# Expert tiles of 128 rows in a fused attention and mixture-of-experts kernel, with the first layer two tiles ahead

## The chip, the cores and the metric

The kernel runs on one core of a Trainium2 chip. The metric is the device time of one execution in microseconds (us), as the median of the runs shown. All data are fp32.

The core has five engines, each with its own instruction queue: TensorE (matmul, here PE, its weight loads PEld), VectorE (DVE), ScalarE (ACT), GpSimd (POOL) and SyncE (SP, which here issues transfers). They meet only through semaphores. Steps that a queue does itself (a wait, register arithmetic, a load of a register from memory) are listed in the trace under names such as DVEq.

## The reference, cut to what matters

The input x is (32, 256, 128). A linear-attention layer with a layer norm comes first, then a mixture of experts with a second layer norm:

```python
x = layernorm(x + attention(x, ...))
x_flat = x.reshape(8192, 128)
shared_out = relu(x_flat @ shared_w1 + b1) @ shared_w2 + b2        # 128 -> 512 -> 128
top_vals, top_idx = top_k(x_flat @ router_w + expert_bias, 2)
weights = softmax(top_vals)
comb = zeros((8192, 16)).at[rows, top_idx].add(weights)
for e in range(16):
    y_e = relu(x_flat @ w1[e] + b1[e]) @ w2[e] + b2[e]             # 128 -> 512 -> 128
    routed_out += comb[:, e:e+1] * y_e
x = layernorm(x + shared_out + routed_out)
```

## The kernel before, in words

**Three stages.** The first (0 to about 525 us) runs the attention, the router and the shared expert over 16 units of 512 tokens in a software pipeline whose order is written out by hand for each engine. GpSimd scatters each token's row twice, once for each chosen expert, into `dispatched_rows` in HBM, grouped by expert (L955). At its end VectorE's `make_table` turns the counts into a table of tiles: for each tile its expert (`tile_ei`) and its first row (`tile_ri`). The second, the **expert stage** (about 525 to 837 us), applies the experts tile by tile. The third (to the end) gathers the two results of each token, adds them and normalizes.

**A tile of the expert stage.** `ST` = 256 rows of one expert are a tile, in `SUB` = 2 halves of 128. Each expert's rows are rounded up to whole tiles, so there are always `ETILES` = 16384 / 256 + 16 = 80. For tile j:

- SyncE `load_rows` (L279 to L285) loads its rows into one of `RING` = 8 buffers: a `value_load` of the first row, then one DMA. It issues two tiles at a time once their earlier scatters are done.
- TensorE `e_turn` (L589) transposes it into PSUM; VectorE `e_xT` (L1269) copies that to SBUF.
- VectorE `e_w1` (L1273) reads the tile's expert number with a `value_load` (L1274) and copies that expert's first-layer weights and bias (128 x 516) into a ring of `W_RING` = 4, so that the matmuls and activations have fixed addresses.
- TensorE `e_up` (L595): 4 matmuls over 256 columns. ScalarE `e_hid` (L839): 4 activations, ReLU with bias, from PSUM to `hide`.
- TensorE `e_down` (L605): a `value_load` of the expert (L607), then 8 matmuls over 128 columns, 4 accumulated for each half.
- VectorE `e_y` (L1280): a `value_load` (L1281), a wait for `e_down` (L1282, L1283), then adds the bias b2. ScalarE `e_weigh` (L847) multiplies by the routing weight. GpSimd (L974 to L980) scatters the rows to `expert_results`, one indirect DMA for each half.

**The order.** Each engine's queue goes through its work in the order written. TensorE takes in step j: `e_turn`(j+2), `e_up`(j+1), `e_down`(j). ScalarE: `e_hid`(j+1), `e_weigh`(j). VectorE: `e_xT`(j+2), `e_w1`(j+3), `e_y`(j), in a loop of 4 steps; the last 4 tiles are written out after it. A `nop` with `nofuse` behind a wait keeps the wait a step of its own in the queue, which stops there; other waits ride on the instruction that follows.

Of the kernel before, what the change touches and what calls it, by code (L numbers as in the profile page):

```python
# [1411 lines left out]
```

## Time and profile before

| | us |
|---|---|
| median of 3 runs (range) | 891.84 (891.44 to 893.44) |
| the profiled execution, its own time | 892.41 |
| its span, first to last instruction | 890.3 |

The profile is of one execution. The span is a little shorter than the time. A row of the timeline gives the start, the time on the engine and, in brackets, how long the engine had been idle before it and what ended this. "issue" as the reason means that the engine waited for nothing that the profile shows. An fp32 matmul appears as two passes. Where a row carries a count, its time runs from the start of the first to the end of the last.

### The profile page before, as it was taken

To read this page: it belongs to the slowest core of one execution; us is meant where nothing else is said; L and a number is where in the kernel's file an instruction comes from. 1 tells how busy PE (TensorE), PEld (TensorE's weight loads), DVE (VectorE), ACT (ScalarE), POOL (GpSimd) and SP (SyncE) were. 2 spreads that over 40 slices of the span, in tenths; PEclk is the share of its full clock that TensorE was granted. 3 is DMA by queue.
4 is the path that set the end of the run, shared out by engine and by line. 5 is a ranking of instruction groups with operands and counts; after the bars stand their busy time and mean duration, and the time that the engine had idled before them with its cause. 6 is when DMAs were issued, how large, how long until landed. Compare 5 with 4: busy or idle time off the path is not lost. (4 is left out here: it accounts for less than half of the span.)

```text
span 890.3 us, 24269 instructions
## 1 busy us (share of the span) xinstructions
PE 785.1 (88%) x8068; PEld 568.6 (64%) x8069; DVE 494.6 (56%) x1496; ACT 489.7 (55%) x1153; POOL 556.4 (62%) x709
## 2 busy tenths in 40 slices
PE   4687999999999999999988769999999999999492
PEld 1243555555565556655555549999999999999340
DVE  2435777788787887788874423333333333333076
ACT  2343666556665567556663306666666666666247
POOL 5334687888878888788887534555555555555344
PEclk9966999999999999999998769999999999999796
DMA  4001012211122102221016221222222222221394
GB/s 164 24 2 43 19 47 65 68 53 31 54 69 64 53 26 62 68 62 56 26 39 204 87 69 41 73 71 67 72 69 65 65 66 63 67 67 40 114 316 138
DMA packets 70388, 63.44 MB, mean 71 GB/s; under 512 B 8066, under 2 KB 61704, under 8 KB 70176
## 3 DMA queue, kind: packets, MB, share of 16 engines
q1 hardware_dynamic: 60816, 44.99, 17.7%
q0 software_dynamic: 9216, 17.07, 5.8%
q8 instruction: 52, 0.85, 0.4%
q14 instruction: 32, 0.26, 0.1%
q10 hardware_dynamic: 272, 0.26, 0.1%
HBM read 38.75 MB, written 25.63 MB: 72 GB/s over the span
## 5 line engine op out<-in xcount | busy, mean ns | idle before, releaser
L979 POOL DMA_INDIRECT expert_results<-yw_all,rows x160 | 157.2, 983 | 155.2 <-ACT yw_all L851 130.5
L843 ACT ACTIVATE hide<-psB,w_ring 128x256 f32<-128x256 f32 x320 | 125.6, 475 | 65.1 <-PE psB L601 65.1
L612 PEld LDWEIGHTS psO<-w_sb,hide 128*128 128x128 f32 x1280 | 155.3, 192 | 4.6 <-issue 0.6
L612 PE MATMUL psO<-w_sb,hide 128*128 x1280 | 156.0, 275 | 0.1
L601 PE MATMUL psB<-x1T,w_ring 128*128 128x256 f32 x640 | 153.1, 382 | 0.2 <-DVE x1T L1271 0.2
L955 POOL DMA_INDIRECT dispatched_rows<-rows,slot x128 | 126.3, 986 | 38.8 <-issue 30.3
L1284 DVE TENSOR_TENSOR K<-psO,b_sb 128x256 f32<-128x256 f32 x80 | 34.0, 425 | 170.9 <-PE psO L612 170.9
L601 PEld LDWEIGHTS psB<-x1T,w_ring 128*128 128x128 f32 x640 | 116.4, 192 | 13.3 <-issue 0.6
L933 POOL TENSOR_TENSOR w_ring<-w_ring,tot 128x128 f32<-128x128 f32 (+2 forms) x160 | 116.8, 750 | 0.0
L851 ACT ACTIVATE yw_all<-K,rows 128x128 f32<-128x128 f32 x160 | 55.4, 393 | 67.5 <-DVE K L1284 67.5
L806 ACT ACTIVATE hide<-psO,cols 128x512 f32<-128x512 f32 x64 | 43.6, 682 | 75.6 <-PE psO L537 75.3
L537 PE MATMUL psO<-x1T,mats 128*128 128x512 f32 x128 | 73.2, 656 | 12.9 <-ACT hide L806 12.9
L1023 DVE SCALAR_TENSOR_TENSOR psP<-psP,cols,delta 128x512 f32<-128x512 f32 x80 | 60.3, 754 | 43.3 <-PE psP L328 43.3
L544 PEld LDWEIGHTS psO<-mats,hide 128*128 128x128 f32 x512 | 64.0, 204 | 20.5 <-issue 14.9
L544 PE MATMUL psO<-mats,hide 128*128 128x128 f32 x512 | 69.8, 294 | 2.2 <-ACT hide L806 2.2
L1034 DVE TENSOR_TENSOR mixed<-psP,hT 128x512 f32<-128x512 f32 x80 | 55.3, 692 | 15.0 <-PE psP L319 6.5
L940 POOL TENSOR_TENSOR o_rstd<-o_var,minus_half 128x16 f32<-128x16 f32 x16 | 46.9, 2931 | 26.8 <-DVE o_var L1077 26.8
L920 POOL TENSOR_TENSOR tot<-tot 128x128 f32<-128x128 f32 (+4 forms) x80 | 22.0, 275 | 62.5 <-ACT R_near L693 34.1
L439 PEld LDWEIGHTS psB<-w_ring,K 64*32 64x32 f32 x2048 | 20.5, 109 | 51.1 <-issue 49.5
L1278 DVE COPY w_ring<-w_sb 128x516 f32 x80 | 34.3, 429 | 29.8 <-issue 29.8
L439 PE MATMUL psB<-w_ring,K 64*32 64x64 f32 x2048 | 30.5, 229 | 20.2 <-POOL w_ring L933 20.0
L328 PE MATMUL psP<-adapt1a,mats 32*128 32x512 f32 x128 | 39.9, 700 | 6.6 <-issue 2.6
(173 smaller groups left out, 1314.9 us busy)
## 6 DMA issues: line engine op xcount, KB each, us to landing
rows<-dispatched_rows SPq DMA_DIRECT2D x80, 132.0 KB, 2.2
w_sb<-expert_results SPq DMA_DIRECT2D x8, 1024.0 KB, 11.9
h_res<-in_hidden SPq DMA_DIRECT2D x16, 256.0 KB, 3.4
out<-w_sb SPq DMA_DIRECT2D x16, 256.0 KB, 2.3
hT<-in_hidden_t SPq DMA_DIRECT2D x15, 256.0 KB, 3.9
w_sb<-in_w SPq DMA_DIRECT2D x14, 256.0 KB, 3.8
expert_results<-yw_all,rows POOLq DMA_INDIRECT x160, 2.3
dispatched_rows<-pad_rows SPq DMA_DIRECT2D x17, 132.0 KB, 3.7
```

The source lines that it names most:

```text
L439: last = mm(to, k, r, start=True, stop=True, tile_position=(64 * b, 32 * c4))
L537: mm(O1, mat("shared_w1")[:, c * 128:(c + 1) * 128], x1T[u % 2][:, :], start=True, stop=True).then_inc(sem(f"hid_ps{c}"))
L544: last = mm(O1[:, j * 128:(j + 1) * 128], hid[:, c, j * 128:(j + 1) * 128], mat("shared_w2")[:, c * 128:(c + 1) * 128], start=(c == 0), st ...
L601: last = mm(up_ps(p)[:, c // 2, (c % 2) * ST:(c % 2 + 1) * ST], w1b[i % W_RING][:, c * 128:(c + 1) * 128], xTe[p], start=True, stop=True)
L612: last = mm(psO[:, p, s * 128:(s + 1) * 128], hide[p][:, c, s * 128:(s + 1) * 128], w2_sb[:, bass.ds(e, 1), c, :].rearrange("p e c -> p (e ...
L843: last = A(hide[p][:, c, :], psB[:, 2 * p + c // 2, (c % 2) * ST:(c % 2 + 1) * ST], ACT.Relu, bias=w1b[i % W_RING][:, HIDDEN + c:HIDDEN + ...
L851: last = A(yw[i][:, s, :], ye[p][:, s, :], ACT.Copy, scale=row_in[i][:, s, AT_W:AT_W + 1])
L933: last = G.tensor_tensor(r, r, l, ALU.mult)
L955: G.indirect_dma_start(rows_dram[:, :], bass.IndirectOffsetOnAxis(slot[u % 2][:, j, k:k + 1], 0), rows[k][u % 2][:, j, :], None).then_inc( ...
L979: G.indirect_dma_start(back_dram[:, :], bass.IndirectOffsetOnAxis(row_in[i][:, s, AT_DEST:AT_DEST + 1].bitcast(u32), 0), yw[i][:, s, :], N ...
L1023: V.scalar_tensor_tensor(ps, ps, col(f"x_bias{n}"), delta[:, :, :], ALU.add, ALU.mult).then_inc(sem(f"mul{n}"))
L1034: V.tensor_tensor(mixed[MIX_BUF[n]][:, :, :], unflat(psP[MIX_BANK[n]]), hT[u % 2][:, :, 1:T + 1], ALU.add).then_inc(sem(f"mixed{n}"))
```

## The change

`ST` becomes 128, so a tile has one half, and there are 16384 / 128 + 16 = 144 tiles in place of 80. `RING` is 16, so the ring holds as many rows as before; rows are loaded, and their scatters counted, in groups of `GROUP` = 4 tiles. TensorE's order is now `e_turn`(j+3), `e_up`(j+2), `e_down`(j), ScalarE's `e_hid`(j+2), `e_weigh`(j); `hide`, `xTe` and `ye` have 4 buffers, and each tile's first layer has a PSUM bank of its own. ScalarE does three of the four chunks of the ReLU; the fourth is done by VectorE in a new `e_hid` behind ScalarE's three, with a semaphore of its own, `e_hid_v`, for which `e_down` and `e_w1` wait too. VectorE's order is `e_xT`(j+3), `e_w1`(j+4), `e_y`(j), `e_hid`(j+2). The table of tiles has two columns of 72 in place of one of 80, the padding rows written to HBM are 128 for each expert, and the load of b2 counts on the semaphore `late_weights`. The core of the diff (left out: shapes of the table's tiles and constants, the pads, that semaphore):

```diff
@@ -23,9 +23,9 @@
 NC = T // L
 HALVES = [2, 4, 8, 16]
 GROUPS = UB * NH // 2
-ST = 256
-SUB = ST // 128
-RING = 8
+ST = 128
+RING = 16
+GROUP = 4
 W_RING = 4
...
@@ -158,15 +158,15 @@
         slot_f = sb("slot_f", [128, TILES, TOPK])
         slot = two("slot", [128, TILES, TOPK], u32)
         dest = sb("dest", [128, TILES, TOPK])
-        hide_both = sb("hide", [128, 2, HC, ST])
-        hide = [hide_both[:, i, :, :] for i in range(2)]
-        hid = hide_both[:, :, :, :].rearrange("p i c t -> p (i c t)").rearrange("p (c t) -> p c t", t=UT)
+        hide_all = sb("hide", [128, 4, HC, ST])
+        hide = [hide_all[:, i, :, :] for i in range(4)]
...
-        tab = sb("tab", [128, 2])
-        yw_all = sb("yw_all", [128, RING, SUB, C])
+        past, past_row = sb("past", [128, 2, EXPERTS]), sb("past_row", [128, 2, EXPERTS])
+        tab = sb("tab", [128, 2, 2])
+        yw_all = sb("yw_all", [128, RING, C])
         tile_ei = sb("tile_ei", [1, ETILES], i32)
         tile_ri = sb("tile_ri", [1, ETILES], i32)
-        row_in = [r[:, i * SUB:(i + 1) * SUB, :] for r in (rows[0][0], rows[1][0], rows[1][1], rows[0][1]) for i in range(2)]
-        xTe = [x1T[0][:, i * ST:(i + 1) * ST] for i in range(2)]
-        ye = [K[i].rearrange("p (s c) -> p s c", c=C) for i in range(2)]
-        yw = [yw_all[:, i, :, :] for i in range(RING)]
+        row_in = [r[:, i, :] for r in (rows[0][0], rows[1][0], rows[1][1], rows[0][1]) for i in range(TILES)]
+        xTe = [x1T[0][:, i * ST:(i + 1) * ST] for i in range(4)]
+        ye = [K[i][:, j * C:(j + 1) * C] for i in range(2) for j in range(2)]
+        yw = [yw_all[:, i, :] for i in range(RING)]
 
...
@@ -278,22 +278,22 @@
 
             def load_rows(j, i):
                 if not (isinstance(j, int) and j < RING):
-                    sp.wait_ge(sem(f"e_back{i // 2}"), (j - i) * (2 * SUB * 16 // RING))
-                for t in range(2):
+                    sp.wait_ge(sem(f"e_back{i // GROUP}"), (j - i) * (GROUP * 16 // RING))
+                for t in range(GROUP):
                     sp.nop(nofuse=True)
                     r = sp.value_load(tile_ri[0:1, bass.ds(j + t, 1)], min_val=0, max_val=EXPERTS * CAP)
-                    sp.dma_start(row_in[i + t], rows_dram[bass.ds(r, ST), :].rearrange("(s p) c -> p s c", p=128)).then_inc(sem(f"e_rows_in{i // 2}"), 16)
+                    sp.dma_start(row_in[i + t], rows_dram[bass.ds(r, ST), :]).then_inc(sem(f"e_rows_in{i // GROUP}"), 16)
             done(sp, "base_out", UNITS - 2)
-            for j in range(0, RING, 2):
-                if j == RING - 2:
+            for j in range(0, RING, GROUP):
+                if j == RING - GROUP:
...
@@ -522,7 +522,8 @@
             def table_turn():
                 pe.wait_ge(sem("tab"), 1)
                 for i in range(2):
-                    last = nc.tensor.transpose(P0[0:1, i * 128:(i + 1) * 128], tab[:, i:i + 1], mat("ident"))
+                    for k in range(2):
+                        last = mm(P0[0:1, (2 * i + k) * (ETILES // 2):(2 * i + k + 1) * (ETILES // 2)], tab[:, i, k:k + 1], mat("ident")[:, 0:ETILES // 2], start=True, stop=True)
                 last.then_inc(sem("tab_ps"))
 
             def f_up(u, c):
...
@@ -584,48 +585,44 @@
             pe.wait_ge(sem("expert_weights"), (UNITS - 1) * 16)
             pe.wait_ge(sem("b2_ready"), 1)
             pe.wait_ge(sem("tile_table"), 1)
-            up_ps = lambda p: psB[:, 2 * p:2 * p + 2, :]
 
             def e_turn(j, i):
-                pe.wait_ge(sem(f"e_rows_in{i // 2}"), (j - i) * (32 // RING) + 32)
-                for s in range(SUB):
-                    last = nc.tensor.transpose(psP[i % 2][:, s * 128:(s + 1) * 128], row_in[i][:, s, 0:C], mat("ident"))
-                last.then_inc(sem("e_turn_ps"))
+                pe.wait_ge(sem(f"e_rows_in{i // GROUP}"), (j - i) * (GROUP * 16 // RING) + GROUP * 16)
+                nc.tensor.transpose(psP[i % 2][:, 0:ST], row_in[i][:, 0:C], mat("ident")).then_inc(sem("e_turn_ps"))
 
             def e_up(j, i):
-                p = i % 2
                 pe.wait_ge(sem("e_xT"), j + 1)
                 pe.wait_ge(sem("e_w1"), j + 1)
                 pe.nop(nofuse=True)
                 for c in range(HC):
-                    last = mm(up_ps(p)[:, c // 2, (c % 2) * ST:(c % 2 + 1) * ST], w1b[i % W_RING][:, c * 128:(c + 1) * 128], xTe[p],
-                              start=True, stop=True)
+                    last = mm(psB[:, i % 4, c * ST:(c + 1) * ST], w1b[i % W_RING][:, c * 128:(c + 1) * 128], xTe[i % 4], start=True, stop=True)
                 last.then_inc(sem("e_up_ps"))
 
             def e_down(j, i):
-                p = i % 2
                 e = pe.value_load(tile_ei[0:1, bass.ds(j, 1)], min_val=0, max_val=EXPERTS - 1)
                 pe.wait_ge(sem("e_hid"), j + 1)
-                pe.nop(nofuse=True)
-                for s in range(SUB):
-                    for c in range(HC):
-                        last = mm(psO[:, p, s * 128:(s + 1) * 128], hide[p][:, c, s * 128:(s + 1) * 128],
-                                  w2_sb[:, bass.ds(e, 1), c, :].rearrange("p e c -> p (e c)"), start=(c == 0), stop=(c == HC - 1))
+                pe.wait_ge(sem("e_hid_v"), j + 1)
+                pe.nop(nofuse=True)
+                for c in range(HC):
+                    last = mm(psO[:, i % 2, 0:C], hide[i % 4][:, c, :], w2_sb[:, bass.ds(e, 1), c, :].rearrange("p e c -> p (e c)"),
+                              start=(c == 0), stop=(c == HC - 1))
                 last.then_inc(sem("e_down_ps"))
 
             e_turn(0, 0)
             e_turn(1, 1)
             e_up(0, 0)
+            e_turn(2, 2)
+            e_up(1, 1)
             with pe.Fori(0, ETILES // RING - 1) as ring:
                 for i in range(RING):
-                    e_turn(pe.snap(ring * RING + (i + 2)), (i + 2) % RING)
-                    e_up(pe.snap(ring * RING + (i + 1)), (i + 1) % RING)
+                    e_turn(pe.snap(ring * RING + (i + 3)), (i + 3) % RING)
+                    e_up(pe.snap(ring * RING + (i + 2)), (i + 2) % RING)
                     e_down(pe.snap(ring * RING + i), i)
             for j in range(ETILES - RING, ETILES):
+                if j + 3 < ETILES:
+                    e_turn(j + 3, (j + 3) % RING)
...
@@ -837,28 +834,24 @@
 
 
             def e_hid(j, i):
-                p = i % 2
                 act.wait_ge(sem("e_up_ps"), j + 1)
-                for c in range(HC):
-                    last = A(hide[p][:, c, :], psB[:, 2 * p + c // 2, (c % 2) * ST:(c % 2 + 1) * ST], ACT.Relu,
-                             bias=w1b[i % W_RING][:, HIDDEN + c:HIDDEN + c + 1])
+                for c in range(HC - 1):
+                    last = A(hide[i % 4][:, c, :], psB[:, i % 4, c * ST:(c + 1) * ST], ACT.Relu, bias=w1b[i % W_RING][:, HIDDEN + c:HIDDEN + c + 1])
                 last.then_inc(sem("e_hid"))
 
             def e_weigh(j, i):
-                p = i % 2
                 act.wait_ge(sem("e_y"), j + 1)
-                for s in range(SUB):
-                    last = A(yw[i][:, s, :], ye[p][:, s, :], ACT.Copy, scale=row_in[i][:, s, AT_W:AT_W + 1])
-                last.then_inc(sem("e_yw"))
+                A(yw[i], ye[i % 4], ACT.Copy, scale=row_in[i][:, AT_W:AT_W + 1]).then_inc(sem("e_yw"))
 
             e_hid(0, 0)
+            e_hid(1, 1)
             with act.Fori(0, ETILES // RING - 1) as ring:
                 for i in range(RING):
-                    e_hid(act.snap(ring * RING + (i + 1)), (i + 1) % RING)
+                    e_hid(act.snap(ring * RING + (i + 2)), (i + 2) % RING)
...
@@ -975,9 +967,8 @@
                 for i in range(RING):
                     pool.wait_ge(sem("e_yw"), ring * RING + (i + 1))
                     pool.nop(nofuse=True)
-                    for s in range(SUB):
-                        G.indirect_dma_start(back_dram[:, :], bass.IndirectOffsetOnAxis(row_in[i][:, s, AT_DEST:AT_DEST + 1].bitcast(u32), 0),
-                                             yw[i][:, s, :], None, bounds_check=TRASH - 1, oob_is_err=False).then_inc(sem(f"e_back{i // 2}"), 16)
+                    G.indirect_dma_start(back_dram[:, :], bass.IndirectOffsetOnAxis(row_in[i][:, AT_DEST:AT_DEST + 1].bitcast(u32), 0),
+                                         yw[i], None, bounds_check=TRASH - 1, oob_is_err=False).then_inc(sem(f"e_back{i // GROUP}"), 16)
 
...
@@ -1266,42 +1259,49 @@
             dve.wait_ge(sem("b2_ready"), 1)
 
 
-            def e_xT(j, p):
+            def e_xT(j, i):
                 dve.wait_ge(sem("e_turn_ps"), j + 1)
-                V.tensor_copy(xTe[p], psP[p][:, 0:ST]).then_inc(sem("e_xT"))
+                V.tensor_copy(xTe[i % 4], psP[i % 2][:, 0:ST]).then_inc(sem("e_xT"))
 
             def e_w1(j, i):
                 e = dve.value_load(tile_ei[0:1, bass.ds(j, 1)], min_val=0, max_val=EXPERTS - 1)
                 if not (isinstance(j, int) and j < W_RING):
                     dve.wait_ge(sem("e_hid"), j + (1 - W_RING))
+                    dve.wait_ge(sem("e_hid_v"), j + (1 - W_RING))
                 dve.nop(nofuse=True)
                 V.tensor_copy(w1b[i % W_RING][:, :], w1_sb[:, bass.ds(e, 1), :].rearrange("p e n -> p (e n)")).then_inc(sem("e_w1"))
 
-            def e_y(j, p):
+            def e_hid(j, i):
+                dve.wait_ge(sem("e_hid"), j + 1)
+                c = HC - 1
+                V.tensor_scalar(hide[i % 4][:, c, :], psB[:, i % 4, c * ST:(c + 1) * ST], w1b[i % W_RING][:, HIDDEN + c:HIDDEN + c + 1], 0.0,
+                                ALU.add, ALU.max).then_inc(sem("e_hid_v"))
+
+            def e_y(j, i):
                 e = dve.value_load(tile_ei[0:1, bass.ds(j, 1)], min_val=0, max_val=EXPERTS - 1)
                 dve.wait_ge(sem("e_down_ps"), j + 1)
                 dve.nop(nofuse=True)
-                V.tensor_tensor(ye[p], psO[:, p, 0:ST].rearrange("p (s c) -> p s c", c=C),
-                                b2_sb[:, bass.ds(e, 1), :].broadcast_to([128, SUB, C]), ALU.add).then_inc(sem("e_y"))
+                V.tensor_tensor(ye[i % 4], psO[:, i % 2, 0:C], b2_sb[:, bass.ds(e, 1), :].rearrange("p e c -> p (e c)"), ALU.add).then_inc(sem("e_y"))
 
             dve.wait_ge(sem("w1_in"), 4 * 16)
-            for j in range(3):
+            for j in range(W_RING):
                 e_w1(j, j)
-                if j < 2:
+                if j < 3:
                     e_xT(j, j)
+            e_hid(0, 0)
+            e_hid(1, 1)
             with dve.Fori(0, ETILES // W_RING - 1) as quad:
                 for i in range(W_RING):
-                    dve.wait_ge(sem("e_up_ps"), quad * W_RING + (i + 1))
-                    e_xT(dve.snap(quad * W_RING + (i + 2)), i % 2)
-                    e_w1(dve.snap(quad * W_RING + (i + 3)), (i + 3) % W_RING)
-                    e_y(dve.snap(quad * W_RING + i), i % 2)
+                    e_xT(dve.snap(quad * W_RING + (i + 3)), i + 3)
+                    e_w1(dve.snap(quad * W_RING + (i + 4)), i)
+                    e_y(dve.snap(quad * W_RING + i), i)
+                    e_hid(dve.snap(quad * W_RING + (i + 2)), i + 2)
             for j in range(ETILES - W_RING, ETILES):
+                if j + 3 < ETILES:
+                    e_xT(j + 3, j + 3)
+                e_y(j, j)
                 if j + 2 < ETILES:
-                    dve.wait_ge(sem("e_up_ps"), j + 1)
-                    e_xT(j + 2, j % 2)
-                if j + 3 < ETILES:
-                    e_w1(j + 3, (j + 3) % W_RING)
-                e_y(j, j % 2)
+                    e_hid(j + 2, j + 2)
 
 
             def f_add(u):
```

## Rows read from the trace of the kernel before

**Rows 1.** The page's first part: busy time, share of the span, instructions.
```profile
PE 785.1 (88%) x8068; PEld 568.6 (64%) x8069; DVE 494.6 (56%) x1496; ACT 489.7 (55%) x1153; POOL 556.4 (62%) x709
```

**Rows 2.** Stages: stretch, us, busy PE, PEld, DVE, ACT, POOL, clock, DMA, GB/s.
```profile
0.00:400.00 400.00, 348.24 (x4717) 204.61 (x4718) 288.27 (x805) 224.05 (x488) 286.87 (x402) 0.96 0.18 54
...
480.00:500.00 20.00, 15.17 (x104) 9.15 (x94) 10.86 (x50) 6.08 (x12) 10.36 (x10) 0.65 0.56 185
...
600.00:700.00 100.00, 100.00 (x698) 94.45 (x698) 32.21 (x80) 60.68 (x162) 52.81 (x54) 1.00 0.24 68
```

**Rows 3.** Groups, 520 to 820 us: count, busy us, mean ns, idle before and releaser.
```profile
L979 POOL DMA_INDIRECT expert_results<-yw_all,rows x151 | 148.4, 983 | 149.2 <-ACT yw_all L851 126.3 <-issue 22.8
...
L843 ACT ACTIVATE hide<-psB,w_ring 128x256 f32<-128x256 f32 x309 | 121.4, 475 | 64.0 <-PE psB L601 64.0
...
L1278 DVE COPY w_ring<-w_sb 128x516 f32 x80 | 34.3, 429 | 29.8 <-issue 29.8
...
L1284 DVE TENSOR_TENSOR K<-psO,b_sb 128x256 f32<-128x256 f32 x76 | 32.3, 425 | 160.9 <-PE psO L612 160.9
```

**Rows 4.** The timeline, TensorE, one tile: start us, us, instruction.
```profile
642.22 0.38 PE L592 MATMUL psP<-mats,rows 128*128 128x128 f32 x2
642.44 1.89 PE L601 MATMUL psB<-x1T,w_ring 128*128 128x256 f32 x8
644.17 1.95 PE L612 MATMUL psO<-w_sb,hide 128*128 x16
645.95 0.38 PE L592 MATMUL psP<-mats,rows 128*128 128x128 f32 x2
```

**Rows 5.** The timeline, VectorE, one turn of its loop.
```profile
601.53 0.42 DVE L1284 TENSOR_TENSOR K<-psO,b_sb 128x256 f32<-128x256 f32 x1 [2.08 <-PE psO L612]
...
602.57 0.43 DVE L1278 COPY w_ring<-w_sb 128x516 f32 x1 [0.28 <-issue]
...
609.00 0.42 DVE L1284 TENSOR_TENSOR K<-psO,b_sb 128x256 f32<-128x256 f32 x1 [2.28 <-PE psO L612]
...
610.47 0.43 DVE L1278 COPY w_ring<-w_sb 128x516 f32 x1 [0.47 <-issue]
612.73 0.42 DVE L1284 TENSOR_TENSOR K<-psO,b_sb 128x256 f32<-128x256 f32 x1 [1.83 <-PE psO L612]
...
613.95 0.43 DVE L1278 COPY w_ring<-w_sb 128x516 f32 x1 [0.47 <-issue]
```

**Rows 6.** VectorE's queue by line, 601.3 to 604 us: ns min/median/max, first and last start.
```profile
L1274 DVEq TENSOR_LOAD <-tile_ei x1: 310/310/310, 601.8 to 601.8; - x1
L1274 DVEq FUSED_REGOPS  x2: 53/122/190, 601.7 to 602.1; - x2
L1281 DVEq TENSOR_LOAD <-tile_ei x1: 302/302/302, 602.7 to 602.7; - x1
L1281 DVEq SEQ_ASSERT  x1: 23/23/23, 603.2 to 603.2; - x1
L1283 DVEq EVENT_SEMAPHORE  x1: 21/21/21, 601.4 to 601.4; - x1
```

**Rows 7.** The timeline at the expert stage's start and end.
```profile
529.17 1.09 PE L592 MATMUL psP<-mats,rows 128*128 128x128 f32 x4 [4.43 <-DMA rows<-dispatched_rows]
...
538.10 0.42 DVE L1284 TENSOR_TENSOR K<-psO,b_sb 128x256 f32<-128x256 f32 x1 [2.50 <-PE psO L612]
...
831.06 0.42 DVE L1284 TENSOR_TENSOR K<-psO,b_sb 128x256 f32<-128x256 f32 x1 [1.69 <-PE psO L612]
...
834.78 0.98 POOL L979 DMA_INDIRECT expert_results<-yw_all,rows  x1 [0.31 <-issue]
836.96 15.57 SPq L300 DMA_DIRECT2D w_sb<-expert_results  x7
```

**Rows 8.** SyncE's row loads by line, 525 to 535 us.
```profile
L285 SPq DMA_DIRECT2D rows<-dispatched_rows x8: 377/378/388, 525.7 to 533.8; - x8
```

**Rows 9.** The chain that ended last: the routing stage's last scatter.
```profile
522.37 2.28 DMA dispatched_rows<-rows,slot
```

More of the change, by code:

```diff
@@ L39 @@
 MIX_BUF = {n: i % 2 for i, n in enumerate(MIX_ORDER)}
-COLS = (["x_mu", "router_b", "xl_b2a", "xl_b2b"] + [f"x_bias{n}" for n in range(NMIX)] + ["w_b", "bonus", "gn_w", "gn_b", "tile_no", "tile_row", "head0", "head1", "head2", "head3"]
+COLS = (["x_mu", "router_b", "xl_b2a", "xl_b2b"] + [f"x_bias{n}" for n in range(NMIX)] + ["w_b", "bonus", "gn_w", "gn_b", "tile_no0", "tile_no1", "tile_row0", "tile_row1", "head0", "head1", "head2", "head3"]
         + [f"shared_b1_{c}" for c in range(HC)])
@@ L246, in _ @@
             load_h(1)
-            sp.dma_start(b2_sb[:, :, :], b2_dram).then_inc(sem("b2_in"), 16)
+            sp.dma_start(b2_sb[:, :, :], b2_dram).then_inc(sem("late_weights"), 16)
             sp.wait_ge(sem("pad_rows"), 1)
             def write_pad(e):
-                sp.dma_start(rows_dram[e * CAP:e * CAP + ST, :].rearrange("(s p) c -> p s c", p=128), pad_rows[:, :, :]).then_inc(sem("padded"), 16)
+                sp.dma_start(rows_dram[e * CAP:e * CAP + ST, :], pad_rows[:, :]).then_inc(sem("padded"), 16)
             write_pad(EXPERTS)
@@ L291, in _ @@
             with sp.Fori(0, ETILES // RING - 1) as ring:
-                for i in range(0, RING, 2):
+                for i in range(0, RING, GROUP):
                     load_rows(sp.snap(ring * RING + (i + RING)), i)
-            for q in range(RING // 2):
-                sp.wait_ge(sem(f"e_back{q}"), ETILES // RING * 2 * SUB * 16)
+            for q in range(RING // GROUP):
+                sp.wait_ge(sem(f"e_back{q}"), ETILES // RING * GROUP * 16)
             for q in range(UNITS // 2):
@@ L894, in _ @@
                     G.memset(rows[k][p][:, :, :], 0.0)
-            G.memset(pad_rows[:, :, :], 0.0)
+            G.memset(pad_rows[:, :], 0.0)
             G.memset(v_flat[0], 0.0)
@@ L1184, in make_table @@
                 link(V.tensor_tensor_scan(tiles_to[:, :], ones_row[:, :], tiles_f[:, :], 0.0, ALU.mult, ALU.add))
-                V.tensor_scalar(past[:, :], tiles_to[:, :], col("tile_no"), None, ALU.is_le)
+                for k in range(2):
+                    V.tensor_scalar(past[:, k, :], tiles_to[:, :], col(f"tile_no{k}"), None, ALU.is_le)
                 link(V.tensor_tensor(first_row[:, 0:EXPERTS], counts[:, :], mat("region"), ALU.add))
@@ L1188, in make_table @@
                 link(V.tensor_tensor(row_step[:, :], first_row[:, 1:EXPERTS + 1], first_row[:, 0:EXPERTS], ALU.subtract))
[L1189 to L1194 removed]
+                link(V.tensor_tensor(past_row[:, :, :], past[:, :, :], row_step[:, :].unsqueeze(1).broadcast_to([128, 2, EXPERTS]), ALU.mult))
+                V.tensor_reduce(tab[:, 0, :], past[:, :, :], AX.X, ALU.add)
+                link(V.tensor_reduce(tab[:, 1, :], past_row[:, :, :], AX.X, ALU.add))
+                V.scalar_tensor_tensor(tab[:, 1, 0:1], tab[:, 1, 0:1], col("tile_row0"), first_row[:, 0:1], ALU.add, ALU.add)
+                link(V.scalar_tensor_tensor(tab[:, 1, 1:2], tab[:, 1, 1:2], col("tile_row1"), first_row[:, 0:1], ALU.add, ALU.add))
+                V.tensor_scalar(tab[:, 0, :], tab[:, 0, :], float(EXPERTS - 1), None, ALU.min)
+                V.tensor_scalar(tab[:, 1, :], tab[:, 1, :], float(EXPERTS * CAP), None, ALU.min).then_inc(sem("tab"))
                 dve.wait_ge(sem("tab_ps"), 1)
                 V.tensor_copy(tile_ei[:, :], P0[0:1, 0:ETILES])
[L1197 removed]
+                V.tensor_copy(tile_ri[:, :], P0[0:1, ETILES:2 * ETILES]).then_inc(sem("tile_table"))
             def c_slots(u):
@@ L1384, in pack @@
     putc("gn_b", g("gn_bias"))
-    putc("tile_no", p.astype(np.float32))
-    putc("tile_row", p.astype(np.float32) * ST)
+    for k in range(2):
+        putc(f"tile_no{k}", (p + k * (ETILES // 2)).astype(np.float32))
+        putc(f"tile_row{k}", (p + k * (ETILES // 2)).astype(np.float32) * ST)
     for n in range(NH):
```

26 lines of the change are left out of this document (8 added, 18 removed).

## Prediction

> **What bounds the kernel now.** I read the page's busy table first: TensorE is busy 785 us of 890, VectorE 495 [rows 1]. A whole-span share says little here, so next comes the table by stage. In the expert stage, 600 to 700 us, TensorE is busy 100.00 of 100 us at granted clock 1.00 and VectorE only 32.21 us [rows 2]. The groups of that stage say who waits: VectorE's L1284 waited 160.9 us for TensorE, ScalarE's L843 64.0 us, and GpSimd's scatter L979 126.3 us for ScalarE [rows 3]. TensorE alone sets the pace. Its timeline shows the pace: from one L592 to the next, 642.22 to 645.95, is 3.73 us for a tile of 256 rows [rows 4]. The first `e_y` starts at 538.10 and the 80th at 831.06, so 79 steps take 292.96 us [rows 7], 3.71 each.
>
> **TensorE's share of the change.** One step splits in rows 4 into 0.22 us for two transposes, 1.73 for the 8 passes of `e_up` over 256 columns (an fp32 matmul is two passes), and 1.78 for the 16 passes of `e_down` over 128 columns: 0.111 us for a pass over 128. The new tile of 128 rows has 1 + 8 + 8 = 17 such passes, 17 x 0.111 = 1.89 us. 144 x 1.89 = 272 us stands against 80 x 3.73 = 298 us: fewer padded rows, 26 us less. If TensorE stayed the bound, that would be the gain. But the tile period falls by half, so I ask what each other engine does once for a tile, whatever its size.
>
> **VectorE's queue, the term that decides.** VectorE's busy time for a new tile is small: 0.43 for the copy of `w1`, and below the 256-column 0.42 each for `e_xT`, `e_y` and the new ReLU, under 1.7 us together [rows 3, 5]. The idle time ahead of L1278 is marked "issue", 29.8 us in 80 [rows 3]: nobody was waited for; the queue itself was busy. I therefore laid out what the queue does for a tile. Clearing the wait of L1283 comes at 601.4, the addition starts at 601.53: 0.16 us with the register step between them (an estimate within the tenths of the rows) [rows 5, 6]. From there to the start of the `w1` copy one step of a loop turn takes 1.04 us, the next as much (not shown), then come 1.47 and 1.22 [rows 5], mean 1.19. They hold the issue of `e_xT` and one `value_load` with its register work: L1274 begins at 601.7, of it 310 ns for the load and 190 ns for the register work behind it [rows 6]. The 1.47 is the step with the loop's branch. From the copy's start (602.57) the second `value_load`, L1281, follows at once and ends with the assertion at 603.2 plus 23 ns [rows 5, 6]; with the gap to the next instruction that is 0.72 us. Sum: 0.16 + 1.19 + 0.72 = 2.07 us that the queue is at work for each tile, none of it dependent on the number of rows. Today it hides in the 3.73 us step, and the queue then stands still 2 us until the next `e_down` is done (idle 1.83 to 2.28 before L1284) [rows 5].
>
> In the changed kernel all of it stays: both `value_load`s, the waits, the loop turn every 4 tiles. Added is the ReLU of the fourth chunk with a wait on a computed count. No row shows that instruction. The nearest is the issue of `e_xT`, an instruction with such a wait: between the addition's start at 601.53 and L1274's first step at 601.7 [rows 5, 6]. That bounds it by 0.10 and 0.20; I take 0.11, since the computed count and the issue are all it adds. From below: zero, if it disappeared in a gap. The wait on `e_up_ps` goes and the second wait of `e_w1` comes, which I put at nothing together (at most one more wait of 21 ns plus its gap, as L1283 in rows 6). So 2.18 us a tile, from 2.07 to 2.40. This is above TensorE's 1.89, so **VectorE's queue becomes the bound** and TensorE waits about 0.3 us in each tile.
>
> Does the order of the work let it run at 2.18? Copying xT(j+2) opens VectorE's step j-1. `e_up` (j+2) can begin about 0.5 us after it, `e_up` and `e_down` take 1.8, so `e_down`(j) is done some 2.5 us after the start of that step; VectorE asks for it in step j, at 2.18 + 0.1 + 0.9 + 0.7 = 3.9. ScalarE has in between one `e_weigh` and three activations, none above the 0.48 of L843's over 256 columns [rows 3], so below 1.9 us in all. So no wait of VectorE's queue comes late, and two tiles of lead are what makes that so. Behind the new ReLU's wait for ScalarE the next `e_xT` is queued, and by this count ScalarE is done a good microsecond before.
>
> **The rest has cover.** GpSimd now scatters once a tile instead of twice: 983 ns plus 0.30 of issue [rows 3, 7] is 1.29, under 2.18. SyncE loads each tile with one DMA; eight take 525.7 to 533.8, 1.16 us each [rows 8], under 2.18; should GpSimd or SyncE be late, each would still have 0.9 us of slack a tile. The rows are refilled in groups of 4 out of 16, which leaves SyncE about 9 tiles between a group's last scatter and its need. The table of tiles has three more small VectorE operations and two more matmuls; SyncE waits for the last scatter of the routing stage (522.37 to 524.65) [rows 9] anyway, so I put them at 0 and at 0.5 us if that cover were gone. Pads of half the size, and the load of `b2` now awaited ahead of the first `c_attn`, are at 0: those ends lie in the first stage, which TensorE fills 87% [rows 2], with tens of microseconds between load and need.
>
> **Ends of the stage.** Start: the first transpose now waits for 4 loads, not 2: 2 x 1.16 = +2.3 us [rows 8]. From first transpose (529.17) to first `e_y` (538.10) are 8.93 us [rows 7]; the new fill has four `w1` copies and three xT ahead of the ReLU, which at 0.75 a pair, half-clock `e_up`s of 1.8 and one queue turn give about 8.0: -0.9. End: from the last `e_y` to the landed last scatter are 831.06 to 836.96, 5.90 us, since GpSimd still owes three scatters [rows 7]. Then, one weighing (0.4, within L843's 0.48), one scatter's delay and its 2.2 us to landing, with 0.4 of backlog: about 4.3, -1.6. Net of the ends: -0.2.
>
> **Sum.** The last four tiles have no `w1` copy and take about 5.0 us together, the 139 before them 139 x 2.18 = 303.0: 308.0 against 292.96, +15.0. With the ends +14.8. The profiled execution took 892.41 us (span 890.3 and 2.1 around it), so 907.2; it stands 0.57 above the median of the runs shown, so I forecast **906.6 us**, 1.6% slower.
>
> **A rule against the row.** L1274's load of a register from SBUF takes 310 ns here and L1281's 302 [rows 6]. The Trainium skill, page "DMA: Bandwidth & Descriptors", section "Latency and other measured facts", gives `tensor_load` a floor of about 600 ns. By that figure, an estimate from the page, the two loads of a tile would add another 0.6 us. The trace disagrees with the page in all steps of the steady stage.
>
> **Rivals.** (A) TensorE stays the bound: the queue work overlaps more than I think, or is issued ahead, and a tile takes 1.89. Then 139 x 1.89 + 4.9 = 267.6, -25.4, with the ends 866. For it speaks that VectorE is busy only a third of the stage; against it that the queue's steps in rows 5 and 6 are strictly one after the other. It decides when the queue's work falls below 1.89. Chance 0.12; another 0.04 lies between 1.89 and 2.06, where the time is still below today's. (B) Slower for more queue work: the ReLU costs 0.20, and the two waits and longer loops add 0.1 more, 2.40 a tile: 139 x 2.40 + 5 = 338.6, 937. It speaks for it that one step in four already takes 0.2 more for no visible reason (613.95 - 612.73 against 1.04) [rows 5]. Chance 0.08. (C) The clock: TensorE's gaps bring it to the low level. Between 480 and 500 it was busy 76% and had a mean clock of 0.65; between 0 and 400 it was busy 87%, as it would be now (1.89 of 2.18), at 0.96 [rows 2]. At 0.96 its step is 1.97, still under 2.18. At the low level it is 3.8; a tenth of the tiles there cost 14 x 1.6 = 22 us more, 929. Chance 0.05. (D) By a mechanism of this kernel, the loads of registers slow down when VectorE works without pause: taking instead of 0.31 us the 0.6 us, 2.78 a tile, gives 139 x 2.78 + 5 = 391, some 990 us. Rows 6 show no sign of it, though VectorE was busy during both loads. This is where the page named above would put it. Chance 0.01.
>
> **How the numbers follow.** Today's time is met at (292.96 + 0.2 - 5) / 139 = 2.07 us a tile. My forecast's own case, 2.07 to 2.36, holds 0.67: 891 to 932. What I call no change (0.2%, about what a measurement of this kernel can tell) is 2.06 to 2.085 and holds 0.03 of all. Faster: A and the stretch under 2.06, 0.16. Slower: 0.81. The range for 8 in 10 takes in a little of the stretch below, and C and the lower part of B above: 890 to 933.
>
> **What would show it.** Right: in the stage VectorE's groups have idle time by "issue", and L1284's successor waits little for TensorE; TensorE is busy near 87% with gaps ahead of the first layer that end on VectorE's xT; the tile period is 2.1 to 2.3 us, with every fourth longer. Wrong: TensorE busy 100% at 1.89 (A); a queue period over 2.4 (B); granted clock under 0.95 (C); register loads far from 305 ns (D); or ScalarE's activations named as what ends the idle time, which would mean that my count of slack in the order of the work is false.

## The result, and the profile after

| | before | after |
|---|---|---|
| median, us (runs) | 891.92 (4) | 906.62 (4), 906.04 to 908.62 |
| ratio, 95% interval | | 1.0166, 1.0145 to 1.0186 |
| profiled execution: time, span | 892.41, 890.3 | 906.18, 904.3 |
| expert stage, first to last `e_y` | 292.96 for 80 tiles | 309.25 for 144 tiles |

The changed kernel is slower by 14.7 us. 906.6 was forecast, in a range of 890 to 933.

I read the stage first, as in [rows 2]. The first line is of the kernel after (stretch, us, busy PE, PEld, DVE, ACT, POOL, clock, DMA, GB/s):

```profile
600.00:700.00 100.00, 97.21 (x776) 90.50 (x775) 54.81 (x184) 53.69 (x184) 45.64 (x46) 1.00 0.21 59
```

By this line alone one would still name TensorE. The groups of the same stretch, VectorE, say otherwise (in [rows 3] L1284 waited for TensorE):

```profile
L1272 DVE COPY w_ring<-w_sb 128x516 f32 x46 | 20.2, 440 | 22.4 <-issue 14.5 <-ACT hide L839 7.9
L1277 DVE TENSOR_SCALAR hide<-psB,w_ring 128x128 f32<-128x128 f32 x46 | 15.7, 342 | 0.0
L1284 DVE TENSOR_TENSOR K<-psO,b_sb 128x128 f32<-128x128 f32 x46 | 13.4, 292 | 22.8 <-issue 22.8
L1264 DVE COPY x1T<-psP 128x128 f32<-128x128 f32 x46 | 13.0, 282 | 0.0
```

All idle time ahead of `e_y` (L1284) is now "issue": it waits neither for TensorE nor for anyone, and the queue comes to it late. VectorE's data path is busy 55% of the time, but its queue sets the pace. Its timeline, a turn of its loop, where [rows 5] showed the one before:

```profile
651.95 0.29 DVE L1284 TENSOR_TENSOR K<-psO,b_sb 128x128 f32<-128x128 f32 x1 [0.57 <-issue]
652.16 0.34 DVE L1277 TENSOR_SCALAR hide<-psB,w_ring 128x128 f32<-128x128 f32 x1
652.42 0.28 DVE L1264 COPY x1T<-psP 128x128 f32<-128x128 f32 x1
653.26 0.43 DVE L1272 COPY w_ring<-w_sb 128x516 f32 x1 [0.56 <-issue]
654.17 0.29 DVE L1284 TENSOR_TENSOR K<-psO,b_sb 128x128 f32<-128x128 f32 x1 [0.48 <-issue]
...
656.15 0.29 DVE L1284 TENSOR_TENSOR K<-psO,b_sb 128x128 f32<-128x128 f32 x1 [0.47 <-issue]
...
658.12 0.29 DVE L1284 TENSOR_TENSOR K<-psO,b_sb 128x128 f32<-128x128 f32 x1 [0.47 <-issue]
...
659.65 0.48 DVE L1272 COPY w_ring<-w_sb 128x516 f32 x1 [0.72 <-ACT hide L839]
660.68 0.29 DVE L1284 TENSOR_TENSOR K<-psO,b_sb 128x128 f32<-128x128 f32 x1 [0.56 <-issue]
```

From one `e_y` to the next are 2.22, 1.98, 1.97 and 2.56 us, mean 2.18. The long one holds the loop's branch. Between the rows the queue is at work: in all 118 tiles of 560 to 820 us the step that clears the wait for TensorE (L1283) starts 48 to 50 ns behind the step before it, where in the kernel before it starts 1.40 to 1.95 us behind. The queue's own lines for 600 to 700 us (ns min/median/max) have about the same durations as [rows 6]:

```profile
L1267 DVEq TENSOR_LOAD <-tile_ei x46: 300/309/402, 599.8 to 698.2; - x46
L1281 DVEq FUSED_REGOPS  x92: 53/122/190, 600.8 to 699.4; - x92
L1281 DVEq TENSOR_LOAD <-tile_ei x46: 298/302/315, 600.9 to 699.1; - x46
L1281 DVEq SEQ_ASSERT  x46: 23/23/23, 601.5 to 699.7; - x46
```

The page's chain that ended last has moved there too:

```profile
PE 37%; issue 15%; DVEq 14%; POOL 13%; DVE 13%; ACT 5%; DMA 2%; SPq 0%; POOLq 0%; ACTq 0%
DVEq L1281 8%; PE psO L545 6%; POOL w_ring L925 6%; PE psP L328 5%; PE psB L439 4%; DVEq L1267 3%; POOL dispatched_rows L947 3%; ACT hide L839 3%; PE psB L481 3%; DVE hide L1277 3%; PE psP L319 3%; DVE K L1284 2%; POOL K L914 2%; PE psP L343 2%; PE psB L459 2%
```

A load of one register (L1281) is the costliest line of the chain, at 8% of the span.

**Why TensorE looks 97% busy.** Its timeline in the kernel after:

```profile
652.30 0.27 PE L591 MATMUL psP<-mats,rows 128*128 128x128 f32 x1
652.84 1.13 PE L598 MATMUL psB<-x1T,w_ring 128*128 128x128 f32 x8 [0.28 <-DVE x1T L1264]
653.82 1.15 PE L607 MATMUL psO<-w_sb,hide 128*128 x8
654.81 0.27 PE L591 MATMUL psP<-mats,rows 128*128 128x128 f32 x1
```

The transpose starts at 652.30 and the first layer at 652.84, 0.54 later, where passes in a row follow at 0.11. The array started nothing for 0.43 us beyond one pass, but of the 0.54 the rows count 0.27 as the transpose, whose end is modelled, and only the rest as idle. The rows that tell are the distances from start to start. The wait ends on VectorE's copy of xT, as forecast.

The ends of the stage, after (for [rows 7]):

```profile
530.12 0.66 PE L591 MATMUL psP<-mats,rows 128*128 128x128 f32 x2 [7.18 <-DMA rows<-dispatched_rows]
...
538.33 0.29 DVE L1284 TENSOR_TENSOR K<-psO,b_sb 128x128 f32<-128x128 f32 x1 [0.85 <-issue]
...
847.59 0.29 DVE L1284 TENSOR_TENSOR K<-psO,b_sb 128x128 f32<-128x128 f32 x1 [0.99 <-PE psO L607]
...
849.13 0.98 POOL L970 DMA_INDIRECT expert_results<-yw_all,rows  x1 [0.30 <-issue]
...
851.33 2.87 SPq L300 DMA_DIRECT2D w_sb<-expert_results  x3
```

### The profile page after: what moved, and what is told of

It reads as the page before. It is cut to its first block, busy times and chain, and to the rows that moved or that the text cites. A ratio compares the mean times of both kernels' runs of the same rounds, so it can differ in the third digit from the quotient of the medians.

```text
span 904.3 us, 27677 instructions
## 1 busy us (share of the span) xinstructions
PE 787.7 (87%) x8442; PEld 570.5 (63%) x8443; DVE 571.0 (63%) x1834; ACT 477.4 (53%) x1249; POOL 542.8 (60%) x693
## 4 chain that ended last, share of the span: by engine, by line
PE 37%; issue 15%; DVEq 14%; POOL 13%; DVE 13%; ACT 5%; DMA 2%; SPq 0%; POOLq 0%; ACTq 0%
DVEq L1281 8%; PE psO L545 6%; POOL w_ring L925 6%; PE psP L328 5%; PE psB L439 4%; DVEq L1267 3%; POOL dispatched_rows L947 3%; ACT hide L839 3%; PE psB L481 3%; DVE hide L1277 3%; PE psP L319 3%; DVE K L1284 2%; POOL K L914 2%; PE psP L343 2%; PE psB L459 2%
## 5 line engine op out<-in xcount | busy, mean ns | idle before, releaser
L970 POOL DMA_INDIRECT expert_results<-yw_all,rows x144 | 143.7, 998 | 184.1 <-ACT yw_all L844 174.0
L598 PE MATMUL psB<-x1T,w_ring 128*128 128x128 f32 x1152 | 160.2, 283 | 8.8 <-DVE x1T L1264 8.1
L607 PE MATMUL psO<-w_sb,hide 128*128 x1152 | 164.4, 286 | 0.4 <-ACT hide L839 0.2
L598 PEld LDWEIGHTS psB<-x1T,w_ring 128*128 128x128 f32 x1152 | 141.2, 193 | 23.8 <-issue 22.3
L607 PEld LDWEIGHTS psO<-w_sb,hide 128*128 128x128 f32 x1152 | 139.5, 191 | 5.8 <-issue 1.2
L844 ACT ACTIVATE yw_all<-K,rows 128x128 f32<-128x128 f32 x144 | 57.9, 402 | 144.8 <-DVE K L1284 144.8
L839 ACT ACTIVATE hide<-psB,w_ring 128x128 f32<-128x128 f32 x432 | 124.5, 357 | 16.9 <-PE psB L598 16.7
L1272 DVE COPY w_ring<-w_sb 128x516 f32 x144 | 63.3, 440 | 69.5 <-issue 44.2
L1284 DVE TENSOR_TENSOR K<-psO,b_sb 128x128 f32<-128x128 f32 x144 | 42.0, 292 | 73.4 <-issue 70.0
L1277 DVE TENSOR_SCALAR hide<-psB,w_ring 128x128 f32<-128x128 f32 x144 | 49.2, 342 | 1.1 <-ACT hide L839 1.0
```

The source lines that it names most:

```text
L598: last = mm(psB[:, i % 4, c * ST:(c + 1) * ST], w1b[i % W_RING][:, c * 128:(c + 1) * 128], xTe[i % 4], start=True, stop=True)
L607: last = mm(psO[:, i % 2, 0:C], hide[i % 4][:, c, :], w2_sb[:, bass.ds(e, 1), c, :].rearrange("p e c -> p (e c)"), start=(c == 0), stop=(c ...
L839: last = A(hide[i % 4][:, c, :], psB[:, i % 4, c * ST:(c + 1) * ST], ACT.Relu, bias=w1b[i % W_RING][:, HIDDEN + c:HIDDEN + c + 1])
L970: G.indirect_dma_start(back_dram[:, :], bass.IndirectOffsetOnAxis(row_in[i][:, AT_DEST:AT_DEST + 1].bitcast(u32), 0), yw[i], None, bounds_ ...
L1272: V.tensor_copy(w1b[i % W_RING][:, :], w1_sb[:, bass.ds(e, 1), :].rearrange("p e n -> p (e n)")).then_inc(sem("e_w1"))
L1277: V.tensor_scalar(hide[i % 4][:, c, :], psB[:, i % 4, c * ST:(c + 1) * ST], w1b[i % W_RING][:, HIDDEN + c:HIDDEN + c + 1], 0.0, ALU.add, A ...
```

## The experiments

The theory: VectorE's queue, at 2.18 us a tile whatever a tile holds, sets the pace. Rivals: TensorE, whose busy share is 97%; ScalarE's chain, which the trace names as one releaser; VectorE's data path or the wait of its new ReLU. The table collects what the traces of all kernels show. The column "a tile" is the mean distance of two `e_y` in the steady part. `e_turn`, `e_up` and `e_down` of a tile are 17 passes of TensorE at 0.11 us, 1.89 us if nothing holds them up.

| kernel | us (runs) | a tile, us | first to last `e_y` |
|---|---|---|---|
| before | 891.92 (4) | 3.73 | 292.96 |
| after | 906.6 (4) | 2.18 | 309.25 |
| held | 865.61 (4) | 1.90 | 268.82 |
| no_load_y | 863.37 (1) | 1.90 | 268.67 |
| relu_act | 892.82 (10) | 2.09 | 296.48 |
| short_down | 906.24 (1) | 2.18 | 308.14 |
| extra_load | 997.00 (1) | 2.82 | 397.95 |
| before_extra_load | 891.73 (10) | 3.73 | 292.97 |
| held_relu_act | 865.27 (4) | 1.90 | 269.05 |
| one_ahead | 868.27 (4) | 1.90 | 271.82 |
| held_short_down | 823.76 (1) | 1.62 | 228.72 |
| before_short_down | 810.84 (1) | 2.72 | 212.38 |

**held: one of the two loads goes.** The expert's number is the same in `e_w1`(j) and `e_y`(j), four steps apart, and the loop has four steps, so a register can carry it.

```diff
+            held = [dve.alloc_register(f"held{i}") for i in range(W_RING)]
...
             def e_y(j, i):
-                e = dve.value_load(tile_ei[0:1, bass.ds(j, 1)], min_val=0, max_val=EXPERTS - 1)
+                e = dve.snap(held[i % W_RING], min_val=0, max_val=EXPERTS - 1)
...
-                e_w1(j, j)
+                dve.reg_mov(held[j], e_w1(j, j))
...
-                    e_w1(dve.snap(quad * W_RING + (i + 4)), i)
+                    e = e_w1(dve.snap(quad * W_RING + (i + 4)), i)
                     e_y(dve.snap(quad * W_RING + i), i)
+                    dve.reg_mov(held[i], e)
```

> The changed kernel, but the expert number that the copy of w1 reads for tile j+4 is kept in one of four registers, and the addition of b2 takes it from there four steps later in place of a load of its own. Queue theory (VectorE's queue sets 2.19 us a tile): a load and its register work, 0.63 to 0.73 us, go, two register moves of about 0.1 together come, so the queue needs 1.6; TensorE's 17 passes of 1.89 us then bound. 139 x (2.19 - 1.89) = 42 us less: 865, from 863 to 872. Rival, VectorE's data path or the wait of its new ReLU for ScalarE is what holds it: no change, 905 to 908. Rival, TensorE is the bound already (its busy share in the stage is 97%): at most 3% of 309 us, 897 or more.

Measured: 865.61 us (863.33 to 866.43), ratio to before 0.9696 (0.9672 to 0.9720). It falls by 41.0 us from the changed kernel, where 42 was worked out. The trace shows TensorE at work without a gap, 1.89 us from transpose to transpose, and now `e_y` waiting for it (the stretch's line, TensorE's timeline, then VectorE's):

```profile
600.00:700.00 100.00, 100.00 (x900) 100.00 (x899) 62.08 (x211) 67.50 (x212) 51.74 (x54) 1.00 0.24 67
```
```profile
652.38 0.27 PE L591 MATMUL psP<-mats,rows 128*128 128x128 f32 x1
652.49 1.06 PE L598 MATMUL psB<-x1T,w_ring 128*128 128x128 f32 x8
653.38 1.06 PE L607 MATMUL psO<-w_sb,hide 128*128 x8
654.27 0.27 PE L591 MATMUL psP<-mats,rows 128*128 128x128 f32 x1
```
```profile
654.64 0.29 DVE L1287 TENSOR_TENSOR K<-psO,b_sb 128x128 f32<-128x128 f32 x1 [0.32 <-PE psO L607]
```

Nothing is left out of this kernel, and it is faster than both given ones, by 26 us and by 41. The edit takes no work from VectorE's data path, from ScalarE, GpSimd or SyncE, and leaves the new ReLU with its wait for ScalarE as it was. So neither the data path nor that wait held the changed kernel at 2.18.

**no_load_y: the same load left out, without the register moves.**

```diff
             def e_y(j, i):
-                e = dve.value_load(tile_ei[0:1, bass.ds(j, 1)], min_val=0, max_val=EXPERTS - 1)
...
-                V.tensor_tensor(ye[i % 4], psO[:, i % 2, 0:C], b2_sb[:, bass.ds(e, 1), :].rearrange("p e c -> p (e c)"), ALU.add).then_inc(sem("e_y"))
+                V.tensor_tensor(ye[i % 4], psO[:, i % 2, 0:C], b2_sb[:, 0, :], ALU.add).then_inc(sem("e_y"))
```

> The changed kernel where the addition of b2 uses expert 0's row for every tile, so that VectorE reads no expert number for it (left out: the bias of the right expert). Queue theory: 1.45 us a tile in the queue, TensorE's 1.89 bounds: 865, from 863 to 870, and as fast as the variant that keeps the number in a register. Rivals as there: no change for VectorE's data path or ScalarE, 897 or more for TensorE.

Measured: 863.37 us in one run; its stage is as long as held's (268.67 against 268.82). With the load gone TensorE bounds both, and the register moves are hidden.

**relu_act: the quarter of the ReLU back on ScalarE.**

```diff
-                for c in range(HC - 1):
+                for c in range(HC):
                     last = A(hide[i % 4][:, c, :], ...)
...
                 pe.wait_ge(sem("e_hid"), j + 1)
-                pe.wait_ge(sem("e_hid_v"), j + 1)
+                if isinstance(j, int) and j + 2 >= ETILES:
+                    pe.wait_ge(sem("e_y"), j - 1)
...
-                    dve.wait_ge(sem("e_hid_v"), j + (1 - W_RING))
...
-                    e_hid(dve.snap(quad * W_RING + (i + 2)), i + 2)
```

The added wait for `e_y` is in the last two tiles alone.

> The changed kernel with the fourth chunk of the ReLU back on ScalarE; VectorE has no ReLU and no wait on it. Queue theory: the issue of the ReLU, its computed count and the second semaphore of the w1 copy go, 0.07 to 0.12 us a tile, 139 times: 890 to 897. ScalarE then works 4 x 0.27 + 0.4 = 1.5 us a tile, still under 2.07. Rival, ScalarE's chain (activations, then weighing) sets the pace: 0.27 us longer a tile, 940. Rival, TensorE: no change, 906.

Measured: 892.82 us, ratio to before 1.0006 (0.9994 to 1.0019): 13.8 us less than the changed kernel, 0.10 us for each of 144 tiles (0.09 by the distances of `e_y`). Moving work from ScalarE to VectorE, with the semaphore that it needs, is what the changed kernel pays these 14 us for. ScalarE with 69% of its time busy sets no pace. The stage's line and VectorE's groups:

```profile
600.00:700.00 100.00, 99.77 (x813) 94.68 (x812) 44.99 (x144) 68.55 (x239) 49.57 (x48) 1.00 0.21 62
```
```profile
L1272 DVE COPY w_ring<-w_sb 128x516 f32 x48 | 20.6, 430 | 28.8 <-issue 28.8
L1284 DVE TENSOR_TENSOR K<-psO,b_sb 128x128 f32<-128x128 f32 x48 | 14.0, 292 | 24.2 <-issue 24.2
```

Here the line has TensorE busy 99.77% and its weight loads 94.68%, yet a tile takes 2.09 us, where 1.89 is what TensorE needs, as held shows. The counts in the same line say it: 813 passes in 100 us here, 900 in held. And the releaser "ACT hide L839" ahead of the copy is gone, with the step that it stood in, the one with the branch, shorter by 0.07 (2.49 against 2.57, medians), though ScalarE now has more to do. In the changed kernel, too, the queue's step that clears the copy's waits (L1271) always starts 46 to 50 ns behind the step before it. ScalarE had been named as the last of several semaphores and did not hold the copy up.

**short_down: TensorE's work cut by a third.**

```diff
-                for c in range(HC):
+                for c in range(HC - 1, HC):
                     last = mm(psO[:, i % 2, 0:C], hide[i % 4][:, c, :], w2_sb[:, bass.ds(e, 1), c, :].rearrange("p e c -> p (e c)"),
-                              start=(c == 0), stop=(c == HC - 1))
+                              start=True, stop=True)
```

> The changed kernel where the second layer multiplies one of its four chunks alone (left out: three quarters of the second layer's products), so TensorE has 11 passes a tile, 1.22 us, in place of 17, 1.89. Queue theory: no change, 904 to 908, since TensorE waits for VectorE. Rival, TensorE (97% busy in the stage) sets the pace: 0.67 us less a tile, 139 times, 813.

Measured: 906.24 us. Six of 17 passes of each tile are left out and the time stays; TensorE's gaps grow instead:

```profile
600.00:700.00 100.00, 74.08 (x505) 61.21 (x506) 54.86 (x183) 53.58 (x184) 45.84 (x46) 1.00 0.20 59
```

The rival that TensorE sets the pace falls.

**extra_load and before_extra_load: the dose the other way.** The same line added to both kernels.

```diff
                 e = dve.value_load(tile_ei[0:1, bass.ds(j, 1)], min_val=0, max_val=EXPERTS - 1)
+                dve.value_load(tile_ei[0:1, bass.ds(j, 1)], min_val=0, max_val=EXPERTS - 1)
```

> The changed kernel with one more load of the expert's number, unused, on VectorE ahead of the addition of b2 in each tile. Queue theory: its full 0.6 to 0.7 us come on top of each tile's 2.18: 144 x 0.65 = 94 us more, 995 to 1005. Rivals (data path, ScalarE, TensorE): hidden, 906.

> The kernel before with the same additional unused load on VectorE ahead of the addition of b2. There the queue stands still 1.8 us a tile, so all theories that name VectorE's queue as covered in the kernel before expect no change: 891 to 893. If the loads disturbed TensorE or the engine's data in another way, each of 80 tiles would show it: up to 80 x 0.65 = 52 us more.

Measured: 997.00 us for the changed kernel, 90.4 more, 0.63 us a tile; 891.73 for the kernel before, ratio 0.9993 (0.9973 to 1.0014), no change. The queue's lines of the added load in extra_load:

```profile
L1282 DVEq TENSOR_LOAD <-tile_ei x35: 297/304/305, 601.7 to 697.9; - x35
L1282 DVEq FUSED_REGOPS  x35: 190/190/190, 602.0 to 698.2; - x35
L1282 DVEq SEQ_ASSERT  x35: 23/23/23, 602.3 to 698.5; - x35
```

304 + 190 + 23 ns and the gaps between make up the 0.63. In the kernel before the queue stands still 1.84 us a tile (median), and with the added load 1.21: the same steps fill part of a wait. This cover for the queue's work is there in the kernel before, and it is what small tiles take away.

**held_relu_act and one_ahead: what the other two parts of the change are worth.** held_relu_act is held with relu_act's edit. one_ahead goes back in addition to one tile of lead on TensorE, ScalarE and VectorE:

```diff
-                    e_turn(pe.snap(ring * RING + (i + 3)), (i + 3) % RING)
-                    e_up(pe.snap(ring * RING + (i + 2)), (i + 2) % RING)
+                    e_turn(pe.snap(ring * RING + (i + 2)), (i + 2) % RING)
+                    e_up(pe.snap(ring * RING + (i + 1)), (i + 1) % RING)
...
-                    e_hid(act.snap(ring * RING + (i + 2)), (i + 2) % RING)
+                    e_hid(act.snap(ring * RING + (i + 1)), (i + 1) % RING)
...
-                    e_xT(dve.snap(quad * W_RING + (i + 3)), i + 3)
+                    e_xT(dve.snap(quad * W_RING + (i + 2)), i + 2)
```

> The variant that keeps the expert number in a register, with the fourth chunk of the ReLU back on ScalarE. There TensorE's 1.89 us a tile is the bound. Queue theory: VectorE's queue falls from about 1.65 to 1.55 us a tile, which is hidden: 865.6 as before, 863 to 868. Rival, ScalarE needs the relief: it then has 4 x 0.27 + 0.4 = 1.5 us of work a tile and waits on two engines in turn; if that chain is longer than 1.89, 2.1 us a tile, 894.

> The same (number kept in a register, ReLU on ScalarE), with the first layer one tile ahead as in the kernel before, in place of two. Between the end of e_up(j) and the start of e_down(j) TensorE still has e_down(j-1), a transpose and e_up(j+1), 1.89 us; ScalarE needs 0.15 + 1.2 for the activations in between. If that holds the second tile of lead is worth nothing: 865, 863 to 868. Rival, with small tiles one tile of lead is too short, since ScalarE gets to the activations late, behind its weighing: TensorE would stand still 0.3 us or more a tile, 907 or more.

Measured: 865.27 us (ratio 0.9693, 0.9669 to 0.9717) and 868.27 us (0.9721, 0.9688 to 0.9753). With TensorE as the bound the ReLU's place is of no account: ScalarE did not need the relief. One tile of lead holds 1.90 us a tile in the steady part. Its stage is 2.8 us longer, of which 1.7 fall on the last four tiles (7.26 against 5.53); the medians' intervals overlap. So two tiles of lead are worth about 3 us by the medians, which these runs can't tell from nothing, and the rival's 40 are excluded.

**before_short_down and held_short_down: the same cut where TensorE is the bound.** The edit is short_down's, in the kernel before on both halves.

> The kernel before where the second layer multiplies one of its four chunks alone (left out: three quarters of the second layer's products): TensorE has 16 - 12 = 4 passes of e_down a tile, 1.34 us less of 3.73. There TensorE is the bound, so the time must fall, until GpSimd's two scatters of 1.29 us a tile bound at 2.6: 79 x (3.73 - 2.6) = 89 us less, 803; down to 787 if GpSimd kept up. The same cut left the changed kernel where it was (906.24). Rival, VectorE's queue or ScalarE already set the pace in the kernel before: no change, 892.

> The variant that keeps the expert number in a register, with the same cut of the second layer (left out: three quarters of its products): TensorE 11 passes, 1.22 us a tile. There the bound is TensorE's 1.89, and beneath it lies VectorE's queue at about 1.55 to 1.7. So a fall to the queue's own time: 139 x (1.894 - 1.62) = 38 us less, 828, from 817 to 838. If nothing but TensorE bounded it, 139 x 0.67 = 93 us less, 772. If the queue still bound it at 1.89, no change, 865.

Measured: 810.84 and 823.76 us, each in one run. The kernel before falls by 81 us, so TensorE did set its pace; I had put the new bound at 2.6 us a tile and it was 2.72. The trace shows the scatters back to back on GpSimd for long stretches, with TensorE waiting for rows at times (us in total, times, longest, 560 to 720 us). That GpSimd is the bound here is read from these rows; no run tests it:

```profile
641.61 0.98 POOL L979 DMA_INDIRECT expert_results<-yw_all,rows  x1 [0.30 <-issue]
642.89 0.98 POOL L979 DMA_INDIRECT expert_results<-yw_all,rows  x1 [0.30 <-issue]
644.18 0.99 POOL L979 DMA_INDIRECT expert_results<-yw_all,rows  x1 [0.30 <-issue]
```
```profile
PEld psP L592 <- DMA rows<-dispatched_rows: 16.9, 26, 2.3
PE psP L592 <- DMA rows<-dispatched_rows: 11.6, 20, 2.1
```

held falls from 1.90 to 1.62 us a tile and no further: that is the time of its queue with one load (2.18 less 0.63, with the moves), where 1.62 was put on record. The 1.22 that TensorE and its 11 passes would have allowed is not reached. The queue again waits for nobody: the steps that clear its waits (L1273, L1286) start 46 to 51 ns behind the ones before them.

## Why the prediction was right

| term | forecast | measured |
|---|---|---|
| a tile | 2.18 | 2.18 |
| first to last `e_y` | +15.0 | +16.3 |
| first load to first transpose | +2.3 | +1.9 |
| first transpose to first `e_y` | -0.9 | -0.7 |
| last `e_y` to the gather | -1.6 | -2.2 |
| before the first load | 0 | -0.9 |
| after the gather | 0 | -0.4 |
| span | +14.8 | +14.0 |

**The queue's work for a tile** was summed from the steps of its own rows: 2.07, and 0.11 for the new ReLU. It is 2.18. The parts of the 0.11 were not quite those that I named. The ReLU with all that hangs on it costs 0.09 to 0.10 (relu_act). Without it the sum from [rows 5, 6] is 2.07, and 2.09 is measured, so the two terms miss by 0.02 each way and cancel. Rival D is excluded: a load takes 298 to 315 ns at L1281 in a queue that never rests. The load with all its register work took 0.63 us in extra_load. The floor of about 600 ns that the Trainium skill gives for `tensor_load` (page "DMA: Bandwidth & Descriptors", section "Latency and other measured facts") doesn't agree with these rows as the time of the load itself; it comes near the 0.63 us of the load with its register work.

**The step over to another bound** is shown from both sides: TensorE's work cut, no change (short_down); the queue's work cut, 41 us less, down to TensorE's 1.89 (held); the queue's work raised, 90 us more (extra_load); the same in the kernel before, nothing (before_extra_load). The 26 us that I gave to TensorE as a gain if it stayed the bound are what held measures against the kernel before. Rival A was thus right on the size, 866, and wrong on its condition.

**Slack in the order of the work** was counted at over a microsecond; one_ahead suggests that there was more than I needed, as even one tile of lead holds a pace of 1.90. My sentence that two tiles of lead are what makes it so is not borne out. one_ahead has the whole ReLU on ScalarE, though; one tile of lead with VectorE's share of the ReLU was not run.

**The start** was 0.4 short of the forecast, by two terms. A load of half the size is issued every 1.11 us, not 1.16 (the first and the ninth are at 524.8 and 533.7, where [rows 8] had the first and the eighth at 525.7 and 533.8); this is the smaller part, 0.1. From the last load that the first transpose waits for to that transpose are 1.94 us (528.18 to 530.12) and were 2.26 (526.91 to 529.17); this 0.3 was not in the sum:

```profile
L285 SPq DMA_DIRECT2D rows<-dispatched_rows x9: 337/338/369, 524.8 to 533.7; - x9
```

**The last four tiles** were put at 5.0 and took 5.75, in steps of 1.15, 1.97, 1.34 and 1.29 us between `e_y`s: without a copy of `w1` TensorE and its hand-over bound the last three (the queue waits 0.5 to 0.8 us ahead of each). That and the 0.6 missed at the end cancel. The stage's other 0.5 is the step, 2.183 in place of 2.18, in 139 tiles. The 0.9 before the first load can't be laid to the change: in the traces here the first load is issued anywhere from 522.6 (held_short_down) to 527.0 (one_ahead), though all run the same first stage but for its pads. That the sum came out within 0.1 us of the median is therefore partly luck. That the step lies near 2.18 and above TensorE's 1.89 is not.

**What I had wrong in the signs to look for:** TensorE's busy share was to fall to 87%. From start to start it does (1.89 of 2.18), but the page shows 97.21, as modelled ends fill short gaps. Anyone who had taken the busy share as the test would have found for rival A. I had also called it a sign of being wrong if ScalarE's activations were named as what ends idle time. They were, for 7.9 of 22.4 us ahead of L1272, and relu_act shows that it meant nothing.

## What to carry to other kernels

Halving a tile halves what is done for each row, and leaves what is done for each tile: count, for every engine's queue, the waits, register loads and branches of a step, and compare their sum with the new step, not the engine's busy time. A number read twice from memory by the same engine is worth a register as soon as the queue is within reach of the bound: here it turned 1.7% slower into 3.0% faster. Moving work to the engine with the lowest busy share can load the one with the fullest queue.
